# Delta-rule decoder kernel: keys first through the front, split loads of half 1, and half 1's query lengths behind the scan's second token

## The reference, cut to what matters

```python
xn = x * rsqrt(mean(x * x) + EPS) * norm1_w
xc = silu(causal_depthwise_conv(xn, conv_w, conv_b))
q = _l2norm((xc @ wq).reshape(b, t, H, HD))
k = _l2norm((xc @ wk).reshape(b, t, H, HD))
v = (xc @ wv).reshape(b, t, H, HD)
beta = sigmoid(xc @ wb); alpha = sigmoid(xc @ wa + GATE_BIAS)
def step(S, inp):
    q_, k_, v_, b_, a_ = inp
    S = a_[..., None, None] * S
    pred = einsum('bhkv,bhk->bhv', S, k_)
    S = S + k_[..., :, None] * (b_[..., None] * (v_ - pred))[..., None, :]
    o = einsum('bhkv,bhk->bhv', S, q_)
    return (S, o)
```

## Time and profile before

| | us |
|---|---|
| median of 3 runs | 1918.45 (1917.17 to 1918.71) |
| profiled execution, whole | 1916.3 |
| its span | 1914.1 |
| PE busy | 1373.1 (72%) |
| DVE busy | 1199.6 (63%) |
| POOL busy | 1005.7 (53%) |
| ACT busy | 755.6 (39%) |

### The profile page before, as it was taken

How to read it: one execution, slowest core, us unless ns; L and a number is a source line. 1 busy time by engine, 2 the same in 40 slices (tenths; PEclk the granted TensorE clock), 3 DMA queues, 4 the chain that set the end, 5 groups by cost and what they waited for, 6 DMA issues and landing times. The chain is left out here.

```text
span 1914.1 us, 28138 instructions
## 1 busy us (share of the span) xinstructions
PE 1373.1 (72%) x6660; PEld 942.6 (49%) x6661; DVE 1199.6 (63%) x3351; ACT 755.6 (39%) x2416; POOL 1005.7 (53%) x1246
## 2 busy tenths in 40 slices
PE   6614558500047766678657899996599999999997
PEld 4413446400035555556546677775355555555554
DVE  4499999999799999999772235344232323222222
ACT  5521224401123766667864688886111111111110
POOL 3258998886589998898765323421111111121211
PEclk9857779855568888889968999997799999999999
DMA  4601114600221101110102112323311501501200
GB/s 123 210 25 34 45 34 142 221 37 0 77 67 33 28 26 38 32 32 24 30 17 89 54 39 63 101 70 123 117 42 61 163 22 40 179 30 62 67 17 6
DMA packets 97684, 125.40 MB, mean 66 GB/s; under 512 B 10001, under 2 KB 74952, under 8 KB 95560
## 3 DMA queue, kind: packets, MB, share of 16 engines
q1 hardware_dynamic: 60040, 97.22, 16.1%
q10 hardware_dynamic: 33136, 18.58, 3.3%
q0 software_dynamic: 4432, 8.73, 1.3%
HBM read 89.68 MB, written 35.74 MB: 66 GB/s over the span
## 5 line engine op out<-in xcount | busy, mean ns | idle before, releaser
L238 POOL TENSOR_TENSOR wt<-wt 128x1024 f32<-128x1024 f32 x128 | 301.3, 2354 | 53.0 <-DVE wt L183 32.4
L244 POOL TENSOR_TENSOR wt<-wt 128x512 f32<-128x512 f32 (+2 forms) x384 | 306.6, 799 | 30.1
L1865 PE MATMUL e_ph<-wt,e_g 128*128 x624 | 274.3, 592 | 0.0
L183 DVE SCALAR_TENSOR_TENSOR wt<-wt,scan 128x256 f32<-128x256 f32 x512 | 240.6, 470 | 0.1
L162 DVE TENSOR_REDUCE wt<-wt 128x16 f32<-128x272 f32 x512 | 217.9, 426 | 0.1
L151 DVE TENSOR_TENSOR wt<-wt,scan 128x256 f32<-128x256 f32 x512 | 208.7, 408 | 10.6 <-PEq L261 10.6
L173 DVE TENSOR_TENSOR scan<-wt,scan 128x256 f32<-128x256 f32 x512 | 213.7, 417 | 0.3
L1356 ACT ACTIVATE wt<-p_pX,p_mx 128x120 f32<-128x120 f32 x512 | 176.4, 387 | 75.1 <-DVE p_mx L1143 74.9
L1758 POOL TENSOR_TENSOR e_ve<-e_mv,eps 128x1 f32<-128x1 f32 x39 | 7.4, 189 | 369.1 <-DVE e_mv L1809 369.1
L1488 PE MATMUL p_pm<-p_w_mix,p_oT 128*128 128x256 f32 x128 | 43.5, 498 | 195.5 <-DMA p_oT<-o 165.6
L1865 PEld LDWEIGHTS e_ph<-wt,e_g 128*128 128x128 f32 x624 | 115.5, 190 | 130.8 <-issue 130.8
(11 more groups left out here) (223 smaller groups left out, 2885.5 us busy)
## 6 DMA issues: line engine op xcount, KB each, us to landing
wt<-in_L_ffn_W SPq DMA_DIRECT2D x24, 1024.0 KB, 5.3
qkv<-f_st ACTq DMA_DIRECT2D x48, 256.0 KB, 2.3
p_kE<-kE SPq DMA_DIRECT2D x16, 480.0 KB, 3.7
p_vP<-vP SPq DMA_DIRECT2D x16, 480.0 KB, 4.5
wt<-qkv SPq DMA_DIRECT2D x6, 1024.0 KB, 9.6
e_xt<-routed ACTq DMA_DIRECT2D x39, 130.0 KB, 2.1
f_xt<-in_x SPq DMA_DIRECT2D x16, 256.0 KB, 2.9
p_oT<-o SPq DMA_DIRECT2D x16, 256.0 KB, 2.9
```

Of the source, the lines that this page charges most:

```text
L183: nc.vector.scalar_tensor_tensor(s["S"][:, h, u], s["S"][:, h, (u - 1) % R], s["gate"][:, jb, h, 2, bass.ds(c * R + u, 1)], s["outer"][:], ...
L238: nc.gpsimd.tensor_tensor(x, s["S"][:, h, z * Q:(z + 1) * Q], s["qn"][:, h, z * Q:(z + 1) * Q].rearrange("p t (o d) -> p t o d", o=1).to_b ...
L244: nc.gpsimd.tensor_tensor(x[:, :, :, 0:half], x[:, :, :, 0:half], x[:, :, :, half:2 * half], ALU.add).then_inc(s["o_fold"][h], 1)
L1865: ins = nc.tensor.matmul(ph2[:], g1[:, c // (C1 // 2), c % (C1 // 2)], wt[:, bass.ds(at_b + (W2_AT + c * F2), F2)], start=(c == 0), stop=( ...
```

## The change

- The keys become projection 0 and the queries projection 1: order of weights, of the matmuls, of the evacuations, of the stores.
- The raw loads of a half go k, gates, q, v (before: k, q, gates, v). Half 1 of block 0 is loaded in two pieces, pairs 4 to 6 and pair 7; the gates only with the second. `arrived` adapts the waits to the two pieces.
- The root of a half's lengths is two instructions, keys' and queries' (`ROOT_K`, `ROOT_Q`), and `inverse` is split in `inverse_keys` and `inverse_queries`.
- Block 0, half 1: ACT does keys, gates, gain root, key root, then query squares and query root. DVE does keys, gates, `inverse_keys`, `shares`, starts the scan, and does the query sums behind token 1 and `inverse_queries` behind token 2.
- Block 1: the parts of a half on DVE are six now, in the order keys, queries, gates, `inverse_keys`, `shares`, `inverse_queries`, behind tokens 1, 2, 3, 4, 6 and 7.

```diff
@@ -303,19 +303,21 @@
-        out = [sem(f"f_out_{n}") for n in "qkv"]
+        out = [sem(f"f_out_{n}") for n in "kqv"]
...
+        SPLIT, LANES = (NB // 4 - 1, 1), G * 2 * (H // G)
+        arrived = lambda jb, h: 16 * (jb + 1) + 16 * h * (len(SPLIT) - 1)
...
-        GAIN, ROOT = 1, 2
-        INVERSE, QUERIES, SCALED = 1, 2, 3
+        GAIN, ROOT_K, ROOT_Q = 1, 2, 3
+        INVERSE, SCALED, QUERIES = 1, 2, 3
...
-        rooted = lambda p, what: 2 * p + what
+        rooted = lambda p, what: 3 * p + what
@@ -349,7 +351,7 @@
             def load_weights():
-                for i, name in enumerate(("L0_attn_wq", "L0_attn_wk", "L0_attn_wv")):
+                for i, name in enumerate(("L0_attn_wk", "L0_attn_wq", "L0_attn_wv")):
@@ -361,18 +363,22 @@
             def load_raw(jb, h):
...
-                pairs = M * jb + M // 2 * (h + 1)
-                half = lambda x: x[h * (M // 2):(h + 1) * (M // 2)]
...
-                for i, name, dst in ((1, "k", x["k"]), (0, "q", x["q"]), (3, None, None), (2, "v", x["vo"])):
-
-                    if i == 3:
-                        sp.wait_ge(gates_out[jb], 64 * (pairs - M * jb))
-                        for y in range(2):
-                            sp.dma_start(s["gate"][:, jb, h, 1 + y], half(k["gates"][jb, y]).rearrange("m g q h t -> (m g q h) t")).then_inc(gate_in[h], 16)
-                    else:
-                        sp.wait_ge(out[i], 16 * pairs)
-                        sp.dma_start(dst[:, h], half(k["qkv"][jb, i]).rearrange("m g q (h d) t -> (m g q h) d t", d=HD)).then_inc(raw_in[name][h], 16)
+                sizes = SPLIT if (jb, h) == (0, 1) else (M // 2,)
+                for piece, size in enumerate(sizes):
+                    first = h * (M // 2) + sum(sizes[:piece])
+                    pairs = slice(first, first + size)
+                    lanes = slice(sum(sizes[:piece]) * LANES, sum(sizes[:piece + 1]) * LANES)
+                    for i, name, dst in ((0, "k", x["k"]), (3, None, None), (1, "q", x["q"]), (2, "v", x["vo"])):
+
+                        if i == 3 and piece == len(sizes) - 1:
+                            sp.wait_ge(gates_out[jb], 64 * (first + size))
+                            for y in range(2):
+                                sp.dma_start(s["gate"][:, jb, h, 1 + y], k["gates"][jb, y, h * (M // 2):(h + 1) * (M // 2)]
+                                             .rearrange("m g q h t -> (m g q h) t")).then_inc(gate_in[h], 16)
+                        elif i < 3:
+                            sp.wait_ge(out[i], 16 * (M * jb + first + size))
+                            sp.dma_start(dst[lanes, h], k["qkv"][jb, i, pairs].rearrange("m g q (h d) t -> (m g q h) d t", d=HD)).then_inc(raw_in[name][h], 16)
@@ -440,7 +446,7 @@
-                pool.wait_ge(raw_in["q"][h], 16)
+                pool.wait_ge(raw_in["q"][h], arrived(0, h))
...
             def outputs(c):
@@ -522,50 +528,58 @@
-                def inverse():
+                def inverse_keys():
...
-                    dve.wait_ge(root_done, rooted(p, ROOT))
+                    dve.wait_ge(root_done, rooted(p, ROOT_K))
...
-                    nc.vector.reciprocal(s["in"][jb]["rq"][:, h], roots[:, h, 1]).then_inc(rn_done, 1)
...
-                return partial(sums, 0), partial(sums, 1), gates, inverse, shares
+                def inverse_queries():
+                    dve.wait_ge(root_done, rooted(p, ROOT_Q))
+                    nc.vector.reciprocal(s["in"][jb]["rq"][:, h], roots[:, h, 1]).then_inc(rn_done, 1)
+
+                return partial(sums, 0), partial(sums, 1), gates, inverse_keys, shares, inverse_queries
...
             def begin(jb):
...
-                    dve.wait_ge(raw_in["k"][h], 16 * (jb + 1))
-                    dve.wait_ge(raw_in["v"][h], 16 * (jb + 1))
+                    dve.wait_ge(raw_in["k"][h], arrived(jb, h))
+                    dve.wait_ge(raw_in["v"][h], arrived(jb, h))
...
-            keys, queries, gates, inverse, shares = lengths(0, 0)
+            keys, queries, gates, inverse_keys, shares, inverse_queries = lengths(0, 0)
...
-            inverse()
+            inverse_keys()
...
-            keys, queries, gates, inverse, shares = lengths(0, 1)
+            inverse_queries()
+            keys, queries, gates, inverse_keys, shares, inverse_queries = lengths(0, 1)
...
-            queries()
...
-            inverse()
+            inverse_keys()
...
-            scan_chunk(nc, dve, s, 0, 0)
+            for u in range(R):
+                scan_step(nc, dve, s, 0, 0, u)
+                if u == 1:
+                    queries()
+                if u == 2:
+                    inverse_queries()
...
-                    if u in (1, 2, 4, 6, 7):
+                    if u in (1, 2, 3, 4, 6, 7):
@@ -660,7 +674,7 @@
                 def square(i):
...
-                    act.wait_ge(raw_in[name][h], 16 * (jb + 1))
+                    act.wait_ge(raw_in[name][h], arrived(jb, h))
@@ -669,15 +683,18 @@
-                def root():
-                    act.wait_ge(fold_done, (p + 1) * 8)
-                    nc.scalar.activation(roots[:, h], lens[:, h], ACT.Sqrt, bias=len_eps[:, 0:1]).then_inc(root_done, 1)
-
-                return partial(square, 0), partial(square, 1), gates, gain_root, root
-
-            keys, queries, set_gates, gain_root, root = lengths(0, 0)
+                def root(i):
+                    act.wait_ge(fold_done, (p * 2 + i + 1) * 4)
+                    nc.scalar.activation(roots[:, h, i], lens[:, h, i], ACT.Sqrt, bias=len_eps[:, 0:1]).then_inc(root_done, 1)
+
+                return partial(square, 0), partial(square, 1), gates, gain_root, partial(root, 0), partial(root, 1)
+
+            keys, queries, set_gates, gain_root, key_root, query_root = lengths(0, 0)
...
-            for part in (gain_root, root, *lengths(0, 1)):
+            for part in (gain_root, key_root, query_root):
+                part()
+            keys, queries, set_gates, gain_root, key_root, query_root = lengths(0, 1)
+            for part in (keys, set_gates, gain_root, key_root, queries, query_root):
@@ -708,7 +725,8 @@
-                for part in lengths(1, h):
+                keys, queries, set_gates, gain_root, key_root, query_root = lengths(1, h)
+                for part in (keys, queries, set_gates, gain_root, key_root, query_root):
```

## The result

The changed kernel takes 1923.95 us (median of 20 runs, 1918.70 to 1929.37) against 1917.49 for the kernel before (20 runs). The ratio is 1.0036 with a 95% interval of 1.0030 to 1.0043: 6.9 us slower by the ratio, 6.5 by the medians. The profiled execution has a span of 1920.8 us, 6.7 more than 1914.1. The prediction said +3.6 and a range up to 1925.0, so the direction and the range held and the size was 3 us short: 6.5 measured.

A forecast was written before the change was run, and what follows sets the result against it. The prediction took DVE's pace to bound the first scan, behind a front chain. Its terms -6.9 (earlier start), +3.7 (moved work) and +6.8 (new places) gave +3.6, a median of 1922.05 us, range 1914.9 to 1925.0.

The forecast's parts named there:

- D: End of the first scan, chunks 14 and 15: the parts' new places behind tokens cost DVE +6.8 us.
- Rival 1: Chunks 14 and 15: DVE's gate product gets in before POOL's L238; the change gives -3.7 us, 1914.75; chance 0.17.
- B: Front: the new gate and key chains to the scan meet, so it starts at 95.3, 6.9 us earlier.
- C: First scan's start: query sums and query reciprocal moved behind tokens 1 and 2 cost DVE +3.7 us.
- A: Front: with key order and split load, pair 7's last keys land at 86.5 and last gate store at 87.2.
- free row: Front's stores: the profile row of a 256 KB store alone, which lands in 2.5 us.
- rival 2: Front's end: early loads hold gate stores of pairs 6 and 7, scan starts 98.4 or later, +6.7 us; chance 0.13.
- the loaded end of the bounds: Front's stores: behind 2 MB of loads a 256 KB store lands in 7.2 us, a gate store in 6.0.
- even turns by bytes: Front's DMA queues: key store would land near 81.8 and scan start 0.7 us sooner; the prediction did not adopt it.

The follow-up runs named there:

- the last four kernels: Unsplit load with values ahead of queries; before with half 1's parts last; both together; both with half 0's key load held: 1915.94, 1913.48, 1908.88, 1907.81 us.

## Why the prediction came out as it did

- **D, the parts' new places: right.** Predicted +6.8, measured +6.42 in the changed kernel and again on the old front. Gate products 2.39 and 2.39 (2.4 predicted), L531's counterpart 1.52 and 1.51 (1.6), key sums of chunk 15 4.91 (4.9), share product 0.29 (0.3). Rival 1, DVE first, didn't happen; L238 was ahead by 0.1 us in each of the four cases seen. The Trainium skill (SBUF — State Buffer, SBUF: two separate sides) states that of a VectorE operation with two SBUF inputs and a GpSimd operation the one that starts first keeps the shared port pair for its whole length; the run without read-outs agrees, 0.28 against 2.39.
- **B, the chain: right.** From the first sigmoid to the scan 5.33 us (5.2 predicted).
- **C, the moved work: right.** The query sums took 2.73 with POOL idle; start to chunk 14 lost 3.54 (-3.45 to +0.09) against 3.7.
- **A, the landings: mis-sized, and this is the 3 us.** I took 3.8 us for the key store of pair 7, "nearer to the free row", and it took 6.0. I took 4.0 for the last key load, and it took 5.3. So the keys were back at 90.2 instead of 86.5. On the other chain I had allowed no wait for pair 6's gate stores; they took 6.3 to 7.0 us and ScalarE stood 2.77 us. Pair 7's then went out 2.4 us later than before and took 3.8 to 4.6, and the last landed at 90.9 instead of 87.2. The scan started at 98.78 and not 95.3.
- **What came is rival 2**, at about the size it named: 90.9 against its 90.65, scan start 98.78 against 98.4, +6.5 in all against +6.7. It had a chance of 0.13, and slower by more than 3.84 us, which is what was measured, had 0.38 against 0.50 for no clear change. The direction was right because C and D were; the forecast of the front was not. That the time still fell into the range, 1 us under its upper end, is owed to that end being set just under rival 2 and not to the sum. The comparison without the split (stores 2.4 us and not 6.2, wait gone) shows that the early loads are the cause.
- Rival 2's argument against was that no more than 1 MB is ahead and not 2. It miscounted. The 3/4 MB of keys, out at 74.86, landed only at 80.6, and the 3/4 MB of queries followed at 76.85: some 1.4 MB stood ahead of pair 6's gate stores. The key store of pair 7 found the rest of both, some 0.9 MB, and not the queries alone. The right term was the loaded end of the bounds. The three measured terms are -3.45 + 3.54 + 6.42 = +6.5.
- Packets show when the stores stood. Early loads move 8 KB at a time, stores 512 bytes. Queues, packets, MB and share of the 16 engines from 76.3 to 78.3 us and from 82.8 to 84.8:

```profile
q1 hardware_dynamic: 53, 0.43, 87.4%
...
q10 hardware_dynamic: 956, 0.48, 82.9%
q1 hardware_dynamic: 30, 0.14, 19.7%
```

In the first window a value store (out at 75.52) and gate stores were under way, and their queues (q10 and q0) moved nothing. In the second, with the loads nearly out of the way, q10 moved 0.48 MB in 2 us. Between them it went in bursts: nothing from 76.2 to 79.0, while q1 moved 0.63 MB, then 0.26 MB by 81.0 beside q1's 0.39, and 0.03 MB from 80.5 to 82. So it isn't a matter of even turns by bytes, by which the prediction had the key store land near 81.8 (it landed at 84.8). What sets the turns no run here isolates.

## To carry to other kernels

When work is moved between the instructions of a loop on one engine, look at what the other engine does at the new place. A short product with two SBUF inputs that starts just behind a 2.3 us GpSimd instruction costs that instruction, and its own length says nothing. Large loads issued early are not free for the stores that the last piece depends on: price such stores at the loaded row. Work that no release depends on belongs behind the last release, as far as the cover goes.

## What the hardware showed that I had not expected

The middle of the front isn't repeatable. The store of pair 7's values went out at 81.83 to 82.97 us in three profiles of kernels that load the keys near 50, and at 78.08 to 84.13 in seven keys-first ones (one of which holds its key load to 51.02), with nearly the same instructions before it. Whole times spread too: all but one of the 20 runs of before beside the changed kernel lie in 3.4 us (1915.57 to 1918.98), those of the changed kernel in 10.7. But before's own 29 runs beside the last four kernels lie between 1912.4 and 1923.29, so the spread isn't only the key order's. What sets it is open.

The part behind the block isn't repeatable either, and no edit here touches it. From the block's end (GpSimd's first instruction behind it) to the kernel's end it is 1394.6 us in the profile of before and 1391.3 to 1397.4 in the eight others that compute everything, with nothing to choose between keys first (1392.3 to 1396.0) and not (1391.3 to 1397.4). A spread of 6 us is there even if the front had none, so whole times of single executions can't judge a change of this size.
